# Scatters of routed rows in pairs, rows of 14 blocks ahead of the expert tiles, sums by a tree, the scan ahead of sums

## What is computed

```python
x = x + attn0(layernorm(x))   # 16 heads of 16: short convolution, silu, L2 norm, delta rule (a recurrence), gated out
x = x + ffn0(layernorm(x))    # 32 experts, each token to 8 of them with a weight, plus a shared MLP of width 256
x = x + attn1(layernorm(x))   # state space: delta, h = exp(delta A) h + delta B x (16 states), y = C h + D x
x = x + ffn1(layernorm(x))    # linear layer, inputs and weights rounded to a 6-bit grid in blocks of 32
```

## Time and profile before

| | us |
|---|---|
| median of 3 runs | 3484.9 (3481.51 to 3489.23) |
| the profiled execution | 3488.45 |
| its span, first to last instruction | 3486.3 |
| PE, DVE, ACT, POOL busy | 2697.7, 2293.9, 1639.6, 1154.0 |
| mean granted TensorE clock | 0.864 |

### The profile page before, as it was taken

The page is one execution under the profiler, slowest core; times in us unless marked ns, Lnnn a source line. Parts: engine busy times, 40 slices in busy tenths (PEclk is TensorE's granted clock), DMA queues, the critical chain, the costliest instruction groups (busy, mean ns, idle before and its releaser), DMA issues.

```text
span 3486.3 us, 111586 instructions
## 1 busy us (share of the span) xinstructions
PE 2697.7 (77%) x46192; PEld 1994.9 (57%) x46192; DVE 2293.9 (66%) x5499; ACT 1639.6 (47%) x2953; POOL 1154.0 (33%) x1152
## 2 busy tenths in 40 slices
PE   4578887888888888776168777999978888888666
PEld 2355555555565555555056666777866666666333
DVE  4878888889988889863132222333445777778996
ACT  4455555545555555412033333444536455554442
POOL 0000333323333333322366666555543223223000
PEclk8778888888888888867589999999989999999777
DMA  7000111111111113214168887998897666664521
GB/s 262 8 10 25 64 58 63 52 60 61 66 64 64 65 64 126 91 56 130 64 212 275 263 268 252 304 308 287 296 335 252 222 227 207 232 211 141 207 94 25
DMA packets 216651, 529.15 MB, mean 152 GB/s; under 512 B 37458, under 2 KB 70740, under 8 KB 207828
## 3 DMA queue, kind: packets, MB, share of 16 engines
q1 hardware_dynamic: 151828, 356.79, 31.9%
q0 software_dynamic: 55104, 156.84, 11.9%
q10 hardware_dynamic: 9216, 8.39, 0.8%
HBM read 311.63 MB, written 210.24 MB: 150 GB/s over the span
## 4 chain that ended last, share of the span: by engine, by line
DMA 47%; DVE 14%; issue 13%; PE 12%; POOL 8%; ACT 5%; SPq 0%; POOLq 0%; ACTq 0%; DVEq 0%
DMA scr_xs<-xn_r,idx 37%; DMA scr_ys<-y,idx_t 9%; POOL scr_ys L978 6%; DVE x L1928 3%; POOL scr_xs L968 2%; PE ps L651 2%; PE ps L753 2%; PE ps L713 1%; PE ps L399 1%; DVE tmp L1564 1%; PE ps L764 1%; DVE tu L1567 1%; PE ps L659 1%; DVE conv L1488 1%; PE ps L744 1%
## 5 line engine op out<-in xcount | busy, mean ns | idle before, releaser
L968 POOL DMA_INDIRECT scr_xs<-xn_r,idx x512 | 535.0, 1045 | 1394.8 <-DMA scr_xs<-xn_r,idx 1032.9
L978 POOL DMA_INDIRECT scr_ys<-y,idx_t x636 | 618.8, 973 | 679.5 <-DVE idx_t L1871 213.4
L1878 DVE TENSOR_TENSOR h<-sg,ps 128x256 f32<-128x256 f32 x318 | 133.6, 420 | 781.3 <-ACT sg L1220 780.6
L651 PE MATMUL ps<-xT,wr 128*128 128x256 f32 x2544 | 624.7, 390 | 0.0
L659 PE MATMUL ps<-wr,h 128*128 128x256 f32 x1272 | 351.7, 400 | 241.4 <-ACT y L1228 218.2
L1228 ACT ACTIVATE y<-ps,of_row 128x256 f32<-128x256 f32 x636 | 266.9, 471 | 569.8 <-DMA scr_ys<-y,idx_t 460.6
L651 PEld LDWEIGHTS ps<-xT,wr 128*128 128x128 f32 x2544 | 477.3, 197 | 69.0 <-issue 12.9
L659 PEld LDWEIGHTS ps<-wr,h 128*128 128x128 f32 x1272 | 235.2, 195 | 323.4 <-issue 269.7
L1928 DVE TENSOR_REDUCE x<-yg 128x256 f32<-128x2304 f32 x64 | 261.4, 4098 | 15.3 <-DMA yg<-scr_x 15.3
L469 PE MATMUL ps<-sq,w_proj 128*128 128x512 f32 x512 | 250.2, 625 | 4.4 <-issue 1.6
L1567 DVE TENSOR_TENSOR tu<-tu,tmp 128x60 f32<-128x60 f32 (+14 forms) x480 | 242.7, 506 | 16.5
(11 more groups left out here) (242 smaller groups left out, 4294.5 us busy)
## 6 DMA issues: line engine op xcount, KB each, us to landing
wr<-in_wexp SPq DMA_DIRECT2D x318, 384.0 KB, 4.1
xt<-scr_xs SPq DMA_DIRECT2D x318, 280.0 KB, 4.1
yg<-scr_ys SPq DMA_DIRECT2D x64, 1024.0 KB, 5.9
scr_xs<-zeros SPq DMA_DIRECT2D x128, 280.0 KB, 5.0
scr_ys<-y,idx_t POOLq DMA_INDIRECT x636, 4.1
x_in<-in_x SPq DMA_DIRECT2D x64, 128.0 KB
x_res<-in_x SPq DMA_DIRECT2D x64, 128.0 KB
scr_x<-x_res SPq DMA_DIRECT2D x16, 512.0 KB, 4.1
```

The lines of the kernel that those rows point to most:

```text
L651: last = pe.matmul(ps[:, bank, half * TILE:(half + 1) * TILE], wr[:, t % NW, at:at + EI], xT2[:, t % NH, k, :], start=k == 0, stop=k == G - 1)
L968: nc.gpsimd.indirect_dma_start(xs[int(i >= FIRST)][:, :], bass.IndirectOffsetOnAxis(idx[:, i % NR, c, k:k + 1], 0), xn_r[:, i % NR, c, :], ...
L978: nc.gpsimd.indirect_dma_start(ys[int(t >= NTH[0])][:, :], bass.IndirectOffsetOnAxis(idx_t[:, t % NRT, r:r + 1], 0), y2[:, t % NY, r, :], ...
```

## The change

Four edits.

1. Scatters of routed rows are counted on two semaphores in turn. Scatter number s waits for s-1, unless s is divisible by 3: then for s-2. GpSimd scatters 14 blocks ahead of the tiles instead of 13 (BESIDE = 2) and puts the other 64 scatters behind every third tile (EVERY = 207 // 64 = 3), the last behind tile 191.
2. `route_tiles(t)` does two tiles at once, at even steps, with the same four instructions on twice the elements; the other engines' counts on `s_route` follow.
3. `combine` sums by a tree: additions of 1024, 512 and 256 elements in place, then the residual.
4. scan(i+1) comes right behind the quantization of block i, ahead of the sums of block i+2, for i below 9; for the later ones it stays behind those sums. scan(0) comes before the loop.

```diff
-        s_scat = sem("s_scat")
+        s_scat = [sem(f"s_scat{n}") for n in range(2)]
...
+        def scattered(engine, n):
+            for m in range(2):
+                engine.wait_ge(s_scat[m], 16 * ((n + 1 - m) // 2))
...
                 sent = (NC * i + c) * TOPK + k
-                if sent:
-                    pool.wait_ge(s_scat, 16 * sent)
+                before_it = sent - 1 if sent % 3 else sent - 2
+                if before_it >= 0:
+                    pool.wait_ge(s_scat[before_it % 2], 16 * (before_it // 2 + 1))
...
-            BESIDE = 3
+            BESIDE = 2
+            EVERY = NTH[0] // (BESIDE * NC * TOPK)
...
             for t in range(NT):
                 store_tile(t)
-                if t < BESIDE * NC * TOPK:
-                    send_rows(NB - BESIDE + t // (NC * TOPK), t // TOPK % NC, t % TOPK)
+                n = t // EVERY
+                if t % EVERY == EVERY - 1 and n < BESIDE * NC * TOPK:
+                    send_rows(NB - BESIDE + n // (NC * TOPK), n // TOPK % NC, n % TOPK)
...
+            def route_tiles(t):
                 st = sR
-                dve.wait_ge(s_xt[t % NX], 16 * (t // NX + 1))
-                if t >= NRT:
-                    dve.wait_ge(s_ys[t % NY], 32 * ((t - NRT) // NY + 1))
+                for n in (t, t + 1):
+                    dve.wait_ge(s_xt[n % NX], 16 * (n // NX + 1))
+                    if n >= NRT:
+                        dve.wait_ge(s_ys[n % NY], 32 * ((n - NRT) // NY + 1))
...
-                    if t + 2 < NT:
-                        route_tile(t + 2)
+                    if t % 2 == 0 and t + 2 < NT:
+                        route_tiles(t + 2)
...
-                V.tensor_reduce(x3[:, i % NX3, c, :], yg[:, n % NG].rearrange("p k d -> p d k"), AX.X, ALU.add)\
-                    .then_inc(s_comb, 1)
+                rows = yg[:, n % NG].rearrange("p k d -> p (k d)")
+                k = TOPK
+                while k > 2:
+                    k //= 2
+                    s3.did(V.tensor_tensor(rows[:, 0:k * D], rows[:, 0:k * D], rows[:, k * D:2 * k * D], ALU.add))
+                    s3.wait(dve)
+                row = x3[:, i % NX3, c, :]
+                s3.did(V.tensor_tensor(row, rows[:, 0:D], rows[:, D:2 * D], ALU.add))
+                s3.wait(dve)
+                V.tensor_tensor(row, row, rows[:, TOPK * D:], ALU.add).then_inc(s_comb, 1)
...
+            scan(0)
             for i in range(NB):
-                scan(i)
                 share(1)
...
                 quant_rows(i)
+                if i < FIRST - 2:
+                    scan(i + 1)
                 if i == FIRST - 2:
                     slots(NT)
                 if i + 2 < NB:
                     share(1)
                     combine_between(i + 2, 0, share)
                     combine_between(i + 2, 1, share)
+                if FIRST - 2 <= i < NB - 1:
+                    scan(i + 1)
```

More of the change, by code:

```diff
@@ L232, in network_kernel @@
         y2 = sb("y2", [P, NY, 2, D])
-        hit = sb("hit", [P, 2, TOPK])
-        hit_of = sb("hit_of", [P, 2, 2, TOPK])
+        hit = sb("hit", [P, 4, TOPK])
+        hit_of = sb("hit_of", [P, 4, 2, TOPK])
         of_row = sb("of_row", [P, NRT, 2, 2])
@@ L350, in network_kernel @@
         CHUNKS = NC * NB
-        SENT = 16 * NC * TOPK
+        SENT = NC * TOPK
+        def scattered(engine, n):
+            for m in range(2):
+                engine.wait_ge(s_scat[m], 16 * ((n + 1 - m) // 2))
         block = ctx.enter_context(nc.Block())
@@ L876, in _ @@
             sp.wait_ge(s_ends[0], 16 * E)
-            sp.wait_ge(s_scat, SENT * FIRST)
+            scattered(sp, SENT * FIRST)
             def load_tile(t):
@@ L883, in load_tile @@
                     ring.filled(sp, "T", t - NX)
-                    sp.wait_ge(s_route, t - NX + 1)
+                    sp.wait_ge(s_route, (t - NX) // 2 + 1)
                 sp.dma_start(xt[:, t % NX].rearrange("p r d -> p (r d)"),
@@ L901, in slots @@
                         sp.wait_ge(s_ends[1], 16 * E)
-                        sp.wait_ge(s_scat, SENT * NB)
+                        scattered(sp, SENT * NB)
                     load_tile(t)
@@ L1016, in route_rows @@
                 if p >= NR:
-                    act.wait_ge(s_scat, SENT * (p - NR + 1))
+                    scattered(act, SENT * (p - NR + 1))
                 rows("route", p, xn_r[:, p % NR, :, 0:D], x_res)
@@ L1222, in tile_out @@
             def tile_out(t):
-                act.wait_ge(s_route, t + 1)
+                act.wait_ge(s_route, t // 2 + 1)
                 if t >= NY:
@@ L1691, in positions @@
                 if p >= NR:
-                    dve.wait_ge(s_scat, SENT * (p - NR + 1))
+                    scattered(dve, SENT * (p - NR + 1))
                 for c in range(NC):
@@ L1855, in _ @@
                     tables(on["H"])
-            def route_tile(t):
+            def route_tiles(t):
                 st = sR
-                dve.wait_ge(s_xt[t % NX], 16 * (t // NX + 1))
-                if t >= NRT:
-                    dve.wait_ge(s_ys[t % NY], 32 * ((t - NRT) // NY + 1))
-                said = xt[:, t % NX, :, D:ROW].rearrange("p r (w k) -> p r w k", w=3)
-                st.did(V.tensor_tensor(hit[:], said[:, :, 0, :], place[:, t].unsqueeze(2).broadcast_to([P, 2, TOPK]),
+                for n in (t, t + 1):
+                    dve.wait_ge(s_xt[n % NX], 16 * (n // NX + 1))
+                    if n >= NRT:
+                        dve.wait_ge(s_ys[n % NY], 32 * ((n - NRT) // NY + 1))
+                said = xt[:, t % NX:t % NX + 2, :, D:ROW].rearrange("p t r (w k) -> p (t r) w k", w=3)
+                here = place[:, t:t + 2].rearrange("p t r -> p (t r)")
+                st.did(V.tensor_tensor(hit[:], said[:, :, 0, :], here.unsqueeze(2).broadcast_to([P, 4, TOPK]),
                                        ALU.is_equal))
@@ L1866, in route_tile @@
                 st.did(V.tensor_tensor(hit_of[:], said[:, :, 1:3, :], hit[:].unsqueeze(2)
-                                       .broadcast_to([P, 2, 2, TOPK]), ALU.mult))
+                                       .broadcast_to([P, 4, 2, TOPK]), ALU.mult))
                 st.wait(dve)
-                st.did(V.tensor_reduce(of_row[:, t % NRT], hit_of[:], AX.X, ALU.add))
+                rows = of_row[:, t % NRT:t % NRT + 2].rearrange("p t r w -> p (t r) w")
+                st.did(V.tensor_reduce(rows, hit_of[:], AX.X, ALU.add))
                 st.wait(dve)
-                V.tensor_tensor(idx_t[:, t % NRT], of_row[:, t % NRT, :, 0], spare[:, t % NY], ALU.max).then_inc(s_route, 1)
+                V.tensor_tensor(idx_t[:, t % NRT:t % NRT + 2].rearrange("p t r -> p (t r)"), rows[:, :, 0],
+                                spare[:, t % NY:t % NY + 2].rearrange("p n r -> p (n r)"), ALU.max)\
+                    .then_inc(s_route, 1)
             def tile_step(t):
@@ L1887, in slots @@
                         tile_step(t)
-                    if t + 2 < NT:
-                        route_tile(t + 2)
+                    if t % 2 == 0 and t + 2 < NT:
+                        route_tiles(t + 2)
             p = NB - 1
             tiles = iter(range(NT + LAG))
-            route_tile(0)
-            route_tile(1)
+            route_tiles(0)
             head_sums(p)
```

4 lines of the change are left out of this document (2 added, 2 removed).

## The result

The changed kernel takes **3240.7 us** (median of 4 runs, 3234.8 to 3243.8) against 3487.1 us for the kernel before (median of the 4 runs beside it): 0.930, 95% interval 0.927 to 0.932. The prediction was 3230 us. The profiled execution shown here took 3243.79 us, its span 3241.6 us.

The account below looks back on a forecast made before the run. Bounds: GpSimd's lagging scatters and first-half tiles, TensorE's waits in the interleaved stretch, VectorE in the last. Terms -90 - 60 - 27 - 78 = -255 us, from the 3484.9 us median to 3230 us; range 3140 to 3330.

Parts of the forecast that it names:

- A: Attention stretch: overlapped scatters, 14 blocks ahead of the tiles, keep pace with the indices and end the stall; -90 us.
- B: First-half tiles: 64 scatters in 192 tiles instead of 96 in 96; -60 us, bounds -103 and -12.
- The work for block 15: Choice, positions and tables, which lay beside 4.4 us tiles and now meet 3.5 us tiles; +10 us, an estimate.
- C: Tile stretch: pairs of tiles routed together halve VectorE's small instructions, where it has 68% idle; nothing gained.
- D: Last stretch: tree sums take 2.82 us instead of 4.06, 22 of them on the path; -27 us.
- E: Interleaved stretch: scan ahead of sums removes TensorE's 4.6 us wait and slow matmuls, shorter sums add 21 us; -78 us.
- the sign of being wrong: Interleaved stretch: iterations above 57 us, where 53 us instead of 62 were forecast, would show the prediction wrong.
- R3: Interleaved stretch gives back: row loads and ScalarE's output wait come late; gain there only -35, time 3273 us; 13%.
- R1: Attention stretch: an overlapped scatter costs about 2.7 us, first store at 1758 us, time 3325 us; 12%.
- R2: Attention stretch: no overlap at all, +108 us there, time 3428 us; 5%.
- R4: Whole kernel: all parts cheap, -92, -93, -27 and -120 us, time 3153 us; 6%.
- R5: Attention stretch: overlapped scatters disturb each other and VectorE holds them up; 4.24 us a scatter, time 3809 us; 2%.

Follow-up runs that it names:

- serial_rest: Changed kernel with scatters one at a time, 13 blocks ahead of the tiles and 96 scatters in the first 96 tiles, as before; 3402.2 us, 0.976 of the kernel before.
- sixth: Changed kernel with one scatter in six overlapped instead of one in three; 3288.8 us, 0.942 of the kernel before.
- route_old: Changed kernel with tiles routed one at a time again; 3449.1 us, 0.982 of the kernel before.
- after_again: Changed kernel with no edit, run again as a control; 3444.1 us, 0.983 of the kernel before.
- scan_old: Changed kernel with the scan back at the top of the loop, behind the sums; 3449.3 us, 0.982 of the kernel before.
- reduce_old: Changed kernel with the single reduction back instead of the tree sums; 3463.1 us, 0.987 of the kernel before.
- before_look: The kernel before with no edit, run to have its trace; 3490.4 us.
- group 3: Later runs on the chip of the second group of experiments, with the first measurement's times again; the kernel before took 3487.8 us.
- groups 1 and 2: First eight experiments, four kernels on each of two chips, run while attention and tile stages were slower; the kernel before took 3509.6 and 3509.5 us.
- overlap_only: The kernel before with the overlapped scatters alone, still 13 blocks ahead of the tiles; 3550.4 us, 1.010 of the kernel before.
- no_overlap: Changed kernel with each scatter waiting for the one just before it; 3496.4 us, 0.996 of the kernel before.
- two_flight: Changed kernel with every scatter overlapped, each waiting for the last but one; 3233.8 us, 0.926 of the kernel before.

## Why the prediction came out right

**A, -90 us: -100.4** (-93.6 against serial_rest). The mechanism is as described: scatters now keep up with the indices, the first store follows block 13's, and the long waits of ScalarE and TensorE are gone. The first store came at 1652.5 us, not 1662.5. What was mis-sized is the overlapped scatter, 1.27 us (1.36 in the mean) instead of 1.93: blocks 12 and 13 went at 175.6/64 = 2.74 us (1476.9, their first indices, to 1652.5), where the forecast had 2.90. I had charged the 0.67 us by which the mean scatter exceeds an undisturbed one to the overlapped one too; the intervals in the change, and sixth, show that this excess lies in the wait for a landing, which an overlapped scatter does not have. The Trainium skill, "DMA: Bandwidth & Descriptors" (Anatomy of one DMA), puts most of a DMA's fixed 2 us down to the receipt of the write. The rows agree so far: the 2.1 us of 3.38 that an overlapped scatter saves are the wait for a landing, but they do not part the receipt from the moving of the bytes. The first store can move by more than ScalarE's 92 us of idle time, since ScalarE had filled four buffers by then; what the last stage gains is A and B together, -176.2 us at the first sum (2570.3 to 2394.1) against -150 forecast. The Trainium skill's page "SBUF — State Buffer" (Who interferes with whom) has VectorE instructions with two SBUF inputs contend with GpSimd instructions that read SBUF. VectorE's convolution steps (128x512, two inputs in SBUF) took a mean of 746 ns before and after; in the change the 140 that ran beside a GpSimd instruction took 746 ns and the 148 others 745. These rows show none of it.

A and B are told apart by marks alone: no undisturbed run has the overlap without the 14 blocks and the spread scatters.

**B, -60 us: -75.8.** The last scatter goes 665.8 us behind the first store (1652.5 to 2318.3), 3.47 us for each of 192 tiles; the forecast had 3.50. The work for block 15, put down at +10 us, is not seen as a loss.

**C, nothing: nothing seen.** The whole times of route_old (3449.1 us) and after_again (3444.1) don't differ. From first store to first sum route_old has 855.9 us, and scan_old and reduce_old, of its group and with pairs, 855.4 and 855.8. From scan 0 to scan 10 it has 544.9 us, 2 us outside the 527.5 to 543.0 of kernels with pairs: a gain of some us there is neither shown nor excluded.

**D and E, -27 and -78 us: -74 together** (-53.0 and -20.9; serial_rest -57.3 and -18.7 against before_look's 593.4 and 189.0), and +5.7 ahead of scan 0, which no run explains. The size per sum was right (2.82 predicted, 2.78 measured), and so was the end: 34 us a block. It falls a little short (20 sums at 1.28 us less would be 25.6 us) because VectorE now waits there for ScalarE, 3.0 us in five times in the change. The step that failed is the split of the interleaved stretch. I gave E the scan's wait and the slow matmuls after it, 57 us, and the tree another 21 us on top, as if they were two supplies. The runs show one gain that both draw on: the tree alone takes 61, the scan's place alone 53, both together 61 (in the first profile 53). Each time the same is left, an iteration of 56 to 57 us instead of the 53 predicted, near the 57 us that the prediction named as the sign of being wrong. That is R3 in part: new waits came (the copy of the quantized rows behind four output stores, not the ones that R3 named), and the 53.0 us gained lie nearer to R3's 35 than to the forecast's 78.

A and B were 26 us better than forecast, D and E 31 us worse, the start of the last stage 6 us: the total came within 11 us of the measured time because the errors cancelled. That closeness is luck; the mechanism of A and B is not, and that of E was wrong in what it would add to D.

**The rivals.** R1 falls with sixth, R2 with the pair at 1649.96 us, R4 with the 56 us iterations. **R5** needs a word. It said that overlapped scatters disturb each other and the attention stage, until the kernel is slower. In group 3 and in the first measurement nothing of it is there. In groups 1 and 2 something like it is: in group 1, one chip and one stretch of runs, the first tile load stands at 1660.3 us without overlap and at 1711.4 (reduce_old), 1733.5 (scan_old) and 1758.2 us (route_old) with it, and overlap_only made the kernel before slower (1.010). The mechanism does not look like R5's: the scatters had time to spare (235.4 us of waits for indices between 400 and 1500 us in after_again), the indices came late, 97 to 109 us apart for the first twelve blocks instead of 91 to 102, with TensorE at a lower granted clock. The stretch from 342 to 1400 us of the change first measured, then no_overlap, after_again, two_flight (columns as in rows 2):

```profile
342.00:1400.00 1058.00, 875.60 (x27126) 605.99 (x27125) 939.28 (x2166) 571.74 (x863) 376.81 (x358) 0.86 0.22 75
```

```profile
342.00:1400.00 1058.00, 896.38 (x26134) 607.15 (x26133) 905.54 (x2096) 555.83 (x831) 339.95 (x317) 0.85 0.18 62
```

```profile
342.00:1400.00 1058.00, 882.92 (x24904) 592.91 (x24904) 870.43 (x1993) 525.49 (x791) 351.53 (x334) 0.82 0.19 63
```

```profile
342.00:1400.00 1058.00, 870.96 (x26991) 603.67 (x26991) 934.75 (x2159) 567.91 (x857) 377.38 (x358) 0.87 0.21 74
```

TensorE is about equally busy in all four, but after_again got 24904 matmuls done where the same code got 27126: its matmuls took longer each, at a clock of 0.82, not 0.86. Two_flight, with every scatter overlapped, has 26991 at 0.87, so overlap alone doesn't do it. The groups' condition alone does part of it: no_overlap, the one kernel of them without overlap, has 26134, and its first tile load is 51 us later than serial_rest's 1609.0. With overlap it was 100 to 150 us later. What the condition was, and why overlap should add to it, is open. It is not the chip as such (group 3 ran on that of group 2), and not the pattern of scatters as such (the first measurement had the same).

## What to carry to other kernels

Where a queue of indirect DMAs waits for each landing, letting every n-th go beside its predecessor costs little more than one issue (here 1.27 to 1.36 us instead of 3.38), and it pays just until the producer of the indices sets the pace; work out that point first. Two edits that both shorten the way to the same wait share one gain: price them by what remains when either is in, not by adding. And measure a change of a few per cent at more than one time: this one gave 0.930 and 0.983 with the same code.

## What the runs showed of the hardware that I had not expected

- In groups 1 and 2 a routed-row or tile transfer took longer from issue to landing. The line of the trace for all transfers of `scr_xs` (min, median, max), serial_rest first, then the changed kernel as first measured, then no_overlap and after_again:

```profile
DMA to landing us min/median/max: 2.4/3.8/15.3
```

```profile
DMA to landing us min/median/max: 2.4/4.0/17.8
```

```profile
DMA to landing us min/median/max: 3.5/5.1/12.5
```

```profile
DMA to landing us min/median/max: 3.3/5.3/12.6
```

- SyncE's register moves ahead of a tile load take 29 to 37 ns in the first profiles and in group 3. In groups 1 and 2 they spread, in these two traces from 2 to 724 ns. First the changed kernel, then no_overlap:

```profile
L890 SPq MOVE xt<-scr_xs x318: 29/29/37, 1610.1 to 2963.3; - x159
```

```profile
L890 SPq MOVE xt<-scr_xs x318: 2/29/724, 1660.3 to 3213.3; - x159
```

  So more than the DMAs was disturbed there. The tile stage suffered too: DMA 268 GB/s between 1800 and 2000 us in after_again, 307 in the first measurement.
- A tree of four additions over 8 rows and a residual of 256 columns takes 2.78 us on VectorE where one reduction of 2304 elements takes 4.06 us.
